# Attention of a hybrid layer: key blocks weighed in pairs, denominators summed on GpSimd, six tiles in flight

## The reference, cut to what matters

```python
kqv = (x @ Wqkv + bqkv).reshape(b, s, 3, 16, 32)
q, k, v = kqv[:, :, 0], kqv[:, :, 1], kqv[:, :, 2]
scores = jnp.einsum('bsnh,btnh->bnst', k, q) / math.sqrt(32)
scores = jnp.triu(scores) + -10000.0 * jnp.tril(ones, k=-1)
attn = jax.nn.softmax(scores, axis=2)
out = jnp.einsum('bnkq,bknh->bqnh', attn, v).reshape(b, s, 512)
return out @ Wo + bo
```

## Time and profile before

| | |
|---|---|
| median of 3 runs | 3363.17 us (3362.29 to 3369.84) |
| profiled execution | 3361.41 us, its span 3359.7 us |
| TensorE, weight loads | busy 3051.5 us (91%), 2086.0 us (62%) |
| VectorE | 2211.0 us (66%) |
| ScalarE, GpSimd | 1094.5 us (33%), 753.8 us (22%) |
| chain that ended last | TensorE 77%, VectorE 9%, issue 4%, DMA 4% |

### The profile page before, as it was taken

One profiled execution on the slowest core, in us unless ns is written; L12 is line 12 of the kernel. 1 busy time (PEld: TensorE's weight loads), 2 busy tenths in 40 slices (PEclk: granted clock), 3 DMA queues, 4 the chain that ended last, 5 costly groups with the idle time before them and its releaser, 6 DMA issues.

```text
span 3359.7 us, 59586 instructions
## 1 busy us (share of the span) xinstructions
PE 3051.5 (91%) x20772; PEld 2086.0 (62%) x20772; DVE 2211.0 (66%) x2961; ACT 1094.5 (33%) x1728; POOL 753.8 (22%) x1065
## 2 busy tenths in 40 slices
PE   3599999999879998999978999999997899999998
PEld 3445457777555446777755444777775444577776
DVE  1356667777646667777764666777764566677776
ACT  1123414434113333344311332344421233243441
POOL 3301102333031111233311110133322011113331
PEclk6779999999879999999987999999998799999998
DMA  7422102111122211111121220111112221021111
GB/s 235 139 47 69 45 13 64 51 49 44 46 79 51 58 31 43 52 44 49 35 83 44 63 63 20 51 44 51 42 43 73 54 69 45 13 63 50 49 44 49
DMA packets 160038, 189.48 MB, mean 56 GB/s; under 512 B 43834, under 2 KB 103866, under 8 KB 158074
## 3 DMA queue, kind: packets, MB, share of 16 engines
q1 hardware_dynamic: 155998, 173.74, 18.6%
q0 software_dynamic: 2720, 10.49, 0.8%
q10 hardware_dynamic: 1152, 3.15, 0.4%
HBM read 104.90 MB, written 23.36 MB: 38 GB/s over the span
## 4 chain that ended last, share of the span: by engine, by line
PE 77%; DVE 9%; issue 4%; DMA 4%; SPq 3%; ACT 2%; POOL 1%; ACTq 0%; POOLq 0%; DVEq 0%
PE ps L706 13%; PE ps L708 12%; PE ps L707 12%; PE ps L850 7%; PE ps L815 6%; PE ps L833 5%; PE ps L1006 4%; PE ps L892 3%; PE ps L992 2%; PE ps L751 2%; PE ps L1052 2%; DVE LM L1565 2%; PE ps L1015 2%; DVE mneg L1473 2%; PE ps L716 1%
## 5 line engine op out<-in xcount | busy, mean ns | idle before, releaser
L706 PE MATMUL ps<-uh,win 128*128 128x512 f32 x1536 | 627.2, 408 | 3.2 <-POOL win L1726 2.5
L708 PE MATMUL ps<-uh,win 128*128 128x512 f32 x1536 | 602.9, 393 | 0.0
L707 PE MATMUL ps<-ul,win 128*128 128x512 f32 x1536 | 599.8, 391 | 0.0
L1473 DVE TENSOR_REDUCE mneg<-ps 128x1 f32<-128x128 f32 (+7 forms) x512 | 363.4, 752 | 175.3 <-PE ps L818 169.9
L1182 ACT ACTIVATE PR<-ps 128x1024 f32<-128x1024 f32 (+3 forms) x384 | 310.2, 809 | 407.8 <-PE ps L836 270.3
L706 PEld LDWEIGHTS ps<-uh,win 128*128 128x128 f32 x1536 | 289.4, 188 | 94.7 <-issue 29.6
L850 PE MATMUL ps<-PR,VG 128*32 128x512 f32 (+3 forms) x1536 | 337.0, 515 | 10.8 <-DVE OS L1479 8.3
L852 PE MATMUL ps<-PR,ones 128*32 128x512 f32 (+3 forms) x1536 | 337.0, 515 | 0.0
L1589 DVE TENSOR_TENSOR LM<-ps,LM 128x512 f32<-128x512 f32 x256 | 170.2, 686 | 242.7 <-PE ps L1006 197.2
L708 PEld LDWEIGHTS ps<-uh,win 128*128 128x128 f32 x1536 | 288.8, 188 | 65.2
L707 PEld LDWEIGHTS ps<-ul,win 128*128 128x128 f32 x1536 | 289.9, 189 | 54.6
(11 more groups left out here) (217 smaller groups left out, 5159.7 us busy)
## 6 DMA issues: line engine op xcount, KB each, us to landing
raw<-in_t SPq DMA_DIRECT2D x128, 256.0 KB, 2.8
QS<-EV SPq DMA_DIRECT2D x192, 128.0 KB, 2.4
KS<-EV SPq DMA_DIRECT2D x168, 128.0 KB, 2.4
X<-in_L_attn_b_W_in_dram SPq DMA_DIRECT2D x10, 1024.0 KB, 7.7
in_t<-tiles POOLq DMA_DIRECT2D x10, 1024.0 KB, 8.2
win_raw<-in_L_attn_a_Wqkv_dram SPq DMA_DIRECT2D x34, 256.0 KB, 3.8
X<-in_L_attn_a_x_dram SPq DMA_DIRECT2D x32, 256.0 KB, 4.4
win_raw<-in_t SPq DMA_DIRECT2D x32, 256.0 KB, 2.7
```

The lines of the kernel that those rows point to most:

```text
L706: pe.matmul(dst, hi_l, hi_r, start=first, stop=False)
L707: pe.matmul(dst, hi_l, lo_r, start=False, stop=False)
L708: return pe.matmul(dst, lo_l, hi_r, start=False, stop=last)
L1473: dve.tensor_reduce(mneg[:, hh, t:t + 1], wide(b0)[:, 0:(t + 1) * P], AX.X, ALU.max, negate=True).then_inc(a_max.sem, 1)
```

## The change

The unit order becomes the natural one, and two units of neighbouring key blocks are weighed together: the four groups of 32 rows of bank 6 now hold two blocks by two heads, and no product with ones is left in `weigh`. `PR` holds four units. GpSimd adds the exponentials up over the key blocks into `acc` (in the half of `win_raw` that attention doesn't use), ten steps a pass, and one group of four products with ones (`denominators`) after the first weighing of the next pass sums them over the rows into bank 7. ScalarE copies that to `rec`. VectorE's `take` now copies one block half and adds the other; it takes over the final products (`scale`) and the low part of the weights (`group_lo`) from GpSimd; `invert` and `scale` of a pass come at the end of the next one. The 16 score tiles are laid into ten slots, and units, tiles and the turned maxima share three pairs of banks in the order of `BODY`, `CLOSE` and `OPEN`; each waits for the reader of the job three before it. The maxima are turned and written in two halves, by four DMAs of ScalarE's queue in place of one of SyncE's. `row_product` holds six tiles in flight in this stage, with the last `denominators` after its first tile. SyncE's waits around `stack` are split, and its first two loads for the state-space block wait for the last denominators.

```diff
-ORDER = [(0, 0), (0, 3), (0, 2), (0, 1), (1, 0), (1, 7), (1, 6), (1, 5), (1, 4), (1, 1), (1, 2), (1, 3)]
+ORDER = [(c, s) for c in range(2) for s in range(4 * c + 4)]
+TILES = [[(0, 3, 0), (0, 2, 512), (0, 0, 896)], [(1, 3, 0), (1, 2, 512), (1, 0, 896)],
+         [(0, 4, 0), (0, 1, 640)], [(1, 4, 0), (1, 1, 640)],
+         [(0, 5, 0)], [(1, 5, 0)], [(0, 6, 0)], [(1, 6, 0)], [(0, 7, 0)], [(1, 7, 0)]]
+AT = [[], [("a", 0), ("a", 1)], [("a", 2), ("a", 3), ("a", 4)], [("t", 0), ("a", 5), ("a", 6), ("a", 7)], [("a", 8), ("a", 9)], []]
+TAIL = [("b", 12), ("b", 13), ("t", 1)]
+SUMMED = [1, 1, 2, 3, 4, 4, 5, 6, 7, 8, 9, 10]
...
+def units_of(k):
+    return [("b", 2 * k + 2), ("b", 2 * k + 3)] if k < PAIRED - 1 else []
+BODY = [j for k in range(PAIRED) for j in units_of(k) + AT[k]] + TAIL
+CLOSE = [j for k in range(PAIRED) for j in units_of(k)]
+OPEN = [("a", i) for i in range(5)] + [("t", 0)] + [("a", i) for i in range(5, 10)] + TAIL
...
+self.bank = {j: 2 * ((start + i) % 3) for i, j in enumerate(jobs)}
+self.before = {}
+for i, j in enumerate(jobs):
+    if i >= 3:
+        self.before[j] = (jobs[i - 3], 0)
+    elif earlier:
...
-PR = sb("PR", [P, 2, 2, HB], at=c)
+PR = sb("PR", [P, 4, 2, HB], at=c)
+OS = sb("OS", [P, 2, HB], at=c)
+acc = win_raw[:, 1].rearrange("p w s k n -> p (w s k n)").rearrange("p (c h t) -> p c h t", c=2, h=2)
...
+def slot_free(slots, p, job):
+    if job not in slots.before:
+        return
+    (kind, i), back = slots.before[job]
+    q = p - back
+    if kind == "b":
+        ex.wait(pe, q + i // UNITS, i % UNITS + 1)
+    elif kind == "a":
+        a_max.wait(pe, q + 1, i + 1)
+    else:
+        m_act.wait(pe, q + 1, i + 1)
...
-def weigh(p, hf, u):
-    c, s, t0, n = span(u)
-    at = t0 - c * HB
-    ex.wait(pe, p, u + 1)
-    if s == 0:
-        o_copied.wait(pe, p, c)
-    last = u == UNITS - 1 or ORDER[u + 1][0] != c
-    for hh in range(2):
-        h = (2 * hf + hh) * HS
-        o, r = hf * 64 + hh * HS, (1 - hf) * 64 + hh * HS
-        pe.matmul(ps[o:o + HS, 6, at:at + n], VG[:, s, h:h + HS],
-                  PR[:, u % 2, hh, 0:n], start=(s == 0), stop=last)
-        i = pe.matmul(ps[r:r + HS, 6, at:at + n], ones[:, 0:HS],
-                      PR[:, u % 2, hh, 0:n], start=(s == 0), stop=last)
+def weigh(p, hf, k):
+    ex.wait(pe, p, 2 * k + 2)
+    if k == 0:
+        o_copied.wait(pe, p, 0)
+        vg_done.wait(pe, p, 1)
+    elif k == 2:
+        o_copied.wait(pe, p, 1)
+    for j in range(2):
+        u = 2 * k + j
+        c, s, t0, n = span(u)
+        at = t0 - c * HB
+        for hh in range(2):
+            h, o = (2 * hf + hh) * HS, j * 64 + hh * HS
+            i = pe.matmul(ps[o:o + HS, 6, at:at + n], VG[:, s, h:h + HS],
+                          PR[:, u % 4, hh, 0:n], start=(k in (0, 2)), stop=(k in (1, 5)))
     i.then_inc(pv.sem, 1)
+def denominators(p):
+    summed.wait(pe, p, 10)
+    for c in range(2):
+        for hh in range(2):
+            o = c * 64 + hh * HS
+            i = pe.matmul(ps[o:o + HS, 7, :], ones[:, 0:HS], acc[:, c, hh, :], start=True, stop=True)
+    i.then_inc(den_pe.sem, 1)
...
+def attend(g, hf, first, last):
+    p, occ = b * 8 + g * 2 + hf, b * 4 + g
+    close = last and hf == 1
+    slots = SLOTS_CLOSE if close else SLOTS_BODY
+    for k in range(PAIRED):
+        for job in units_of(k):
+            scores_b(slots, p, p, hf, occ, job)
+        weigh(p, hf, k)
+        if k == 0 and not (first and hf == 0):
+            if hf == 1 and not first:
+                pj_lo.wait(pe, b * 4 + g, 4)
+            denominators(p - 1)
+        if not close:
+            for job in AT[k]:
+                if job[0] == "t":
+                    turn_maxima(slots, p, job[1])
+                else:
+                    scores_a(slots, p, 1 - hf, occ + hf, job[1])
+        if hf == 0 and not last and 1 <= k <= 4:
+            if k == 1 and not first:
+                den_act.wait(pe, p - 1, 1)
+            project(g + 1, k - 1)
+    if not close:
+        for job in TAIL:
+            if job[0] == "t":
+                turn_maxima(slots, p, job[1])
+            else:
+                scores_b(slots, p, p + 1, 1 - hf, occ + hf, job)
...
+6, lambda: denominators(b * 8 + 7))
...
+    m_act.wait(act, p, c + 1)
+    for hh in range(2):
+        act.dma_start(QS[slot][STACK:STACK + 1, hh, c * HB:(c + 1) * HB].bitcast(F32),
+                      mrow[c][hh * HALF:(hh + 1) * HALF, :].bitcast(F32)).then_inc(s_mrow[slot][c], 16)
+def exponential(slots, job, p, u, first):
+    n = span(u)[3]
+    st_pe.wait(act, p, u + 1)
+    if u >= 4:
+        pv.wait(act, p, (u - 4) // 2 + 1)
+        summed.wait(act, p, SUMMED[u - 4])
+    elif not first:
+        pv.wait(act, p - 1, (u + 8) // 2 + 1)
+        summed.wait(act, p - 1, SUMMED[u + 8])
+    bank = slots.bank[job]
+    act.activation(PR[:, u % 4, :, 0:n], ps[:, bank:bank + 2, 0:n], ACT.Exp, scale=SCALE).then_inc(ex.sem, 1)
+def take_denominators(p, first):
+    den_pe.wait(act, p, 1)
+    if not first:
+        o_scaled.wait(act, p - 1, 2)
+    act.copy(rec[:, :], ps[:, 7, :]).then_inc(den_act.sem, 1)
...
+for u in range(UNITS):
+    exponential(slots if u >= 2 else SLOTS_BODY, ("b", u if u >= 2 else UNITS + u), p, u, head)
+    if u == 1:
+        maxima(SLOTS_BODY, p, 1, hf, None if head else occ - 1 + hf)
+        if hf == 0 and not last:
+            group_hi(b * 4 + g + 1)
+    if u == 3 and not head:
+        take_denominators(p - 1, first and hf == 1)
+    if u == 9 and not close:
+        maxima(slots, p + 1, 0, 1 - hf, occ)
...
+def maximum(slots, p, i):
+    a_pe.wait(dve, p, i + 1)
+    for hh, t, at in TILES[i]:
+        m = dve.tensor_reduce(mneg[:, t // HALF, hh, t % HALF:t % HALF + 1], wide(slots.bank["a", i])[:, at:at + (t + 1) * P],
+                              AX.X, ALU.max, negate=True)
+    m.then_inc(a_max.sem, 1)
+def take(p, hf, c, first=False):
+    pv.wait(dve, p, 2 if c == 0 else PAIRED)
+    if c == 0 and not first:
+        o_scaled.wait(dve, p - 2, 2)
+    rows_ = slice(c * 64, (c + 1) * 64)
+    f = P if c == 0 else 0
+    if f:
+        dve.tensor_copy(OS[rows_, hf, 0:f], ps[0:64, 6, 0:f])
+    dve.tensor_copy(OS[rows_, hf, f:HB], ps[64:128, 6, f:HB]).then_inc(s_half, 1)
+    dve.wait_ge(s_half, p * 2 + (c + 1))
+    dve.tensor_tensor(OS[rows_, hf, f:HB], ps[0:64, 6, f:HB], OS[rows_, hf, f:HB], ALU.add).then_inc(o_copied.sem, 1)
+def invert(p, q):
...
+        den_act.wait(dve, p, 1)
+    cols = slice(q * WIN, (q + 1) * WIN)
+    dve.reciprocal(rec[:, cols], rec[:, cols]).then_inc(o_rec.sem, 1)
+def scale(p, g, hf):
+    o_rec.wait(dve, p, 2)
+    o_copied.wait(dve, p, 2)
+    for c in range(2):
+        rows_ = slice(c * 64, (c + 1) * 64)
+        dst = OT[hf * 64:(hf + 1) * 64, g, c * HB:(c + 1) * HB] if isinstance(g, int) else \
+            OT[hf * 64:(hf + 1) * 64, bass.ds(g, 1), c * HB:(c + 1) * HB].rearrange("p a t -> p (a t)")
+        dve.tensor_tensor(dst, OS[rows_, hf, :], rec[rows_, :], ALU.mult).then_inc(o_scaled.sem, 1)
+def group_lo(n):
+    qkw_hi.wait(dve, n, 1)
+    dve.tensor_tensor(win[:, 0, :, 1], win_raw[:, 0, :, 1], win[:, 0, :, 0].bitcast(F32), ALU.subtract).then_inc(qkw_lo.sem, 1)
...
+if hf == 0 and not last:
+    group_lo(b * 4 + g + 1)
+for k in range(1, 5):
+    if not close:
+        for kind, i in AT[k]:
+            if kind == "a":
+                maximum(SLOTS_BODY, p + 1, i)
+    if k == 1:
+        take(p, hf, 0, first)
+    if hf == 0 and not last:
+        project_lo(g + 1, k - 1, False)
+if not head:
+    invert(p - 1, 0)
+take(p, hf, 1)
+if not head:
+    invert(p - 1, 1)
+    scale(p - 1, g if hf == 1 else g - 1, 1 - hf)
...
+    if not first:
+        until(den_pe, p - 1, 1)
+    for u in (1, 2, 3, 5, 6, 7, 8, 9, 10, 11):
+        c, s_, t0, n = span(u)
+        at = t0 - c * HB
+        until(ex, p, u + 1)
+        if u == 1:
+            pool.tensor_copy(acc[:, 0, :, 0:P], PR[:, 0, :, 0:P]).then_inc(s_add, 1)
+            pool.wait_ge(s_add, p + 1)
+            pool.sem_inc(s_tick, 1)
+            i = plus(acc[:, 0, :, P:HB], PR[:, 0, :, P:HB], PR[:, 1, :, 0:n])
+        elif u == 5:
+            i = plus(acc[:, 1], PR[:, 0], PR[:, 1])
+        else:
+            i = plus(acc[:, c, :, at:HB], acc[:, c, :, at:HB], PR[:, u % 4, :, 0:n])
+        i.then_inc(summed.sem, 1)
+        until(summed, p, SUMMED[u])
+def attend(g, hf, first, last):
+    p = b * 8 + g * 2 + hf
+    sums(p, first and hf == 0)
+    if not last:
+        until(pv, p, PAIRED)
+        values(g + 1, hf)
+        until(vg_done, p + 2, 1)
```

More of the change, by code:

```diff
@@ L318, in hybrid_layer @@
         s_kone = sem("s_kone")
+        s_half = sem("s_half")
         s_bias = sem("s_bias")
@@ L890, in _ @@
+                for part in range(3):
+                    with (pe.Fori(1, GROUPS - 1) if part == 1 else ExitStack()) as i_:
+                        g = i_ if part == 1 else (0 if part == 0 else GROUPS - 1)
+                        for hf in range(2):
```

(28 more changed lines are left out.)

289 lines of the change are left out of this document (117 added, 172 removed).

## The result

The kernel after takes 3430.15 us (median of 4 runs, 3419.43 to 3440.37), beside 3366.51 for the kernel before in the same session: the ratio is 1.0195, 95% interval 1.0173 to 1.0217. It is slower. The forecast was 3339, faster than before, with a range of 3265 to 3400. The profiled execution has a span of 3429.4 against 3359.7, 69.7 us more. TensorE's mean granted clock is 0.901 against 0.941. Since only the levels 0.50 and 1.00 occur, (1 - clock) x 2 x span is the time at 0.50: 680 us after, 400 before. "The level" is this granted clock, and a "stand" is time in which TensorE waits for another engine or a DMA.

The account below looks back on a forecast made before the run. TensorE was taken as the bound, GpSimd as nearly free. Passes 1 to 6 -1.6, opening and pass 0 -9.7, pass 7 +5.3 gave -6.0 us a batch, -24 in four: 3339 us, range 3265 to 3400.

Parts of the forecast that it names:

- Weighing on TensorE: Two key blocks by two heads weighed together, 0.99 us per paired weighing; 3.2 us a pass saved on TensorE.
- Sums on GpSimd: GpSimd's copy and adds over key blocks: 17.4 us, with turns and waits 22.3 us a pass, under 26.35.
- A plain pass: Passes 1, 3, 5, 6, without projection: chain of waits of 25.8 us, 26.1 with the port, against 26.35 before.
- rival D: TensorE, idle a quarter of a plain pass, loses the clock's fast level there: 3400 us; chance 0.07.
- A projecting pass: Passes that also project the next group: 34.0 us, 34.4 with the port, against 35.35 before.
- Port: VectorE's two-SBUF-input instructions and GpSimd's SBUF reads exclude each other: 0.3 us a plain, 0.4 a projecting pass.
- Opening and pass 0: Batch start through pass 0: scores start earlier and the clock rises at 1012, -9.7 us a batch.
- Pass 7: Last pass of a batch: TensorE stands 3.8 us for GpSimd's last sum; +5.3 us a batch with slow clock.
- Sum: All terms together: -6.0 us a batch, -24 in four, so 3339 us.
- C: Rival: opening's slow clock stays (-6.0 us a batch) and the port costs its upper ends: 3361 us; chance 0.15.

Follow-up runs that it names:

- e1: Kernel after plus unread filler products at pass starts and, in plain passes, ahead of the second score tile and third weighing: 1.0025 of the kernel before.
- e5: Kernel after plus 7 unread filler products only ahead of the third weighing of plain passes: 1.0089 of the kernel before.
- e6: Kernel after plus unread filler products at pass starts (4) and ahead of plain passes' second score tile (5), none before the third weighing: 1.0149 of the kernel before.
- e14: Kernel before plus one wait in each of passes 1, 3, 5 and 6, ahead of the sixth weighing: 1.0261 of the kernel before.
- e15: Kernel before plus two waits in each of passes 1, 3, 5 and 6, ahead of the fourth and sixth weighing: 1.0324 of the kernel before.
- e7: Kernel after with `take(p,0)` moved one score tile earlier and filler products at pass starts and ahead of the second score tile: 0.9898 of the kernel before.
- e12: Kernel after with `take(p,0)` moved earlier and filler products in the passes, the opening and pass 7: 0.9820 of the kernel before.
- e8: Kernel after with `take(p,0)` moved earlier and the final products replaced by copies, leaving out the division: 0.9970 of the kernel before.

## Why the prediction was wrong, step by step

- **Weighing on TensorE**: right. A paired weighing takes 1.05 us at the full level (0.99 worked out).
- **Sums on GpSimd**: a little cheap. From its timeline in pass 3:

```profile
1115.24 0.50 POOL L1922 COPY win_raw<-PR 128x256 f32<-128x256 f32 x1 [5.63 <-PE ps L916]
1115.92 2.04 POOL L1913 TENSOR_TENSOR win_raw<-PR 128x768 f32<-128x768 f32 x1 [0.18 <-POOL win_raw L1922]
...
1123.96 2.35 POOL L1913 TENSOR_TENSOR win_raw<-win_raw,PR 128x1024 f32<-128x1024 f32 x1 [0.34 <-POOL win_raw L1913]
```

  1024 elements take 2.35 (2.41), the turn from one to the next 0.34 (0.26), and the first add ends 3.0 us after the denominators (2.8). The 768-wide add takes 2.04 here, but 1.82 in passes where it starts later.
- **A plain pass**: the step that failed, and only from its middle on: it took the full level of the clock for granted through TensorE's stands. Up to the third weighing the chain holds: `take(p,0)` forecast to end 7.7 us after the denominators, the third weighing starts 8.1 after them (1114.9 to 1123.02). The rest was worked out at the full level and ran at 0.50. With the level full (e1, e5, and one pass of e6 with its third stand unfilled) pass 3 takes 26.7 us for 26.1: the chain of waits was right and the clock missing, 4.3 us on average in a plain pass of the second batch. The prediction said itself that TensorE's savings turn into waits, found it idle for a quarter of a plain pass, and gave that as rival D; it priced D at 37 us a batch at 0.50 and put its chance at 0.07. Measured are 61 us in the passes and 10 more in pass 7. The passes lost 23 us a batch against the forecast. D was the case. The prediction gives no reason for so low a chance; the kernel before keeps the full level in such a pass, but e14 shows that one stand of 1.24 us more takes it away.
- The Trainium skill, "TensorE: Matmul & The Clock Gate", section "A second HAM failure mode: psum-queue depth-cycling", has it of one kernel that a TensorE which idles briefly and often between groups of products swings between the two levels. The prediction didn't cite it; the kernel after, e14 and e15 agree with it, with stands of 0.9 to 1.9 us. It would have spoken for rival D.
- **A projecting pass**: 35.8 for 34.4. In e7 and e12 it is 34.1 to 34.2 where no time at 0.50 falls in it and 35.7 where 3.4 us do: again the clock.
- **Port**: 0.3 to 0.4 us were put on the path; the first large add takes 0.2 us longer beside the second product, and copies in place of the products (e8) make a plain pass no shorter.
- **Opening and pass 0**: right in the sum, partly by luck. TensorE's last L706 product ahead of the first scores, in the kernel before:

```profile
977.15 0.39 PE L706 MATMUL ps<-uh,win 128*128 128x512 f32 x1
```

  And after (L741 is that line):

```profile
987.40 0.39 PE L741 MATMUL ps<-uh,win 128*128 128x512 f32 x1
```

  The second batch starts 10.25 us later after, so its closing copy at 1044.64 counts as 1034.4; forecast 1035.9, before 1045.56. The level rises at 1018.7, as 1008.4 in that count, some 4 us earlier than put; against that the first score starts 2.5 us later than the 983 it was counted from. In four batches the stretch is 7 to 12 us shorter, 10.2 on average (9.7 forecast), with 24 to 34 us at 0.50.
- **Pass 7**: right. The denominators come 21.5 us in (22 forecast), after a stand of 2.95 (3.8 forecast). TensorE's timeline:

```profile
1266.21 1.06 PE L916 MATMUL ps<-win_raw,ones 128*32 128x512 f32 x8 [2.95 <-POOL win_raw L1913]
1267.21 23.01 PE L969 MATMUL ps<-wo,OT 128*128 128x512 f32 x53
```

  To the eighth addition to `X` it costs 4.7 us a batch for 5.3, with 7 to 14 us at 0.50 in it.
- **Sum**: forecast -24, measured +70 in the profiled execution. Opening and pass 7 came to -22 where -18 was forecast, the unchanged stages to +6 where nothing was, the passes to +86 where -6 was.
- **Rivals**: C's own terms (3.7 us a batch of opening, the port at its upper ends 2.8) give about 3365, not 3361; nothing rests on it.
